# Out-projection of a Mamba-style mixer: three float32r passes from high and low parts in place of plain float32

## Chip, cores and metric
One NeuronCore of one Trainium2 chip runs the whole two-layer model in one launch. The metric is the device time of one launch in microseconds (us), the median of several runs; lower is better.

## What is computed
Two layers over 2 x 1024 tokens of width 256. The change touches one piece, the mixer of layer 0 (64 heads of 64 channels, 8 groups, 128 states). Cut to what matters:

```python
proj = einsum('bld,pd->blp', hidden, W_in)              # gate | x,B,C | dt
hbc  = silu(causal_conv4(x,B,C) + conv_b)
dt   = softplus(dt + dt_bias); A = -exp(A_log)
# per chunk: Y = (C B^T * L) (x dt) + C state * exp(cumsum(dt A));  state = decay * state + B^T (x dt decay)
y    = Y + D * x
g    = y * silu(gate)                                   # (tokens, 4096)
gg   = g.reshape(..., 8, 512); gg = gg * rsqrt(mean(gg*gg, -1) + EPS)
out  = (gg.reshape(..., 4096) * norm_weight) @ W_out.T  # the out-projection, (tokens, 256)
```

## The kernel before
`mixer` (L346 to L794) works group by group (8 groups of 512 channels), and in each group chunk by chunk (16 chunks of 128 tokens), so 128 chunks c. Five engines run five streams of instructions written out by hand, all as one loop over slots c = -5 to 130 (`SLOTS`, L430). In slot c the streams work on chunk c (its inputs), on p = c-1 (its output y) and on e = c-2 (its out-projection). Projection and convolution of x, B and C run ahead in 288 blocks spread over the slots (`fills`): two blocks a slot, three in every fourth slot. A block is 260, 384 or 388 columns wide.

TensorE (L540) in a slot: the state's part of y (L574), the diagonal part (L581), a block (L75 to L77 through `matmul3`), the gate's projection into the bank pgt, then four transposes of x into the bank pxt (L602), B and C (L608, L609), first half of the decay matrix `decays(c, 0)` (L563), state matmul (L619), the last block, `decays(c, 1)`, the out-projection of e (L632) and four transposes of y(p) into pxt (L640). `decays(c, 0)` waits for the rows rl and ll of chunk c, which SyncE loads from DRAM (`cs_in`, L559).

The out-projection: y is turned into pxt, ScalarE copies the bank to gt in float32 (L672), and TensorE multiplies gt by wo, four plain float32 matmuls of 128x128 by 128x256. TensorE carries each out as two instructions in the profile, so 8 a chunk, 1024 in all. VectorE adds the result to the accumulator (L794).

VectorE (L743) in a slot: t1 from the state's part (L748), `finish` of the last block of the slot before (L741), y (L759, it waits for GpSimd's addition L513 to t1), `taps` and `finish` of a block (L734, L741), the gate (L764, L767), the carry (L776), the decay matrix (L784), the last block's taps, the accumulation (L794). Where p is a multiple of 8, L748 is left out and y starts from xd.

GpSimd (L468) in a slot: L513, in slots 4 to 12 of a group one piece of `split` for the next group's weights, then L520, L523, L525, L530, and the two small operations L535 and L537. `split` makes high and low float32r parts of w_raw in pieces 0 to 7; piece 8, in slot 12, writes wo = wo_raw * norm weight into one of two buffers (L490) and raises `wo_split`.

SyncE (L438) is one queue in order. Per chunk it waits until the decays of chunk c-2 are done and issues four small loads, one of rl and three of ll (L462, L464). Ahead of those of chunk 16g+2 it waits for all three of `wx_split`, `wg_split` and `wo_split` of group g and loads the next group's weights, w_raw (1280 KB) and wo_raw (512 KB):

```python
if c % 16 == 2 and g < G0 - 1:      # L455
    sp.wait_ge(wx_split, 2 * (g + 1))
    sp.wait_ge(wg_split, 2 * (g + 1))
    sp.wait_ge(wo_split, g + 1)
    load_weights(g + 1)
```

Of the kernel before, what the change touches and what calls it, by code (L numbers as in the profile page):

```python
# [14 lines left out]
P = 128  # L15
T = 2048
D = 256
# [328 lines left out]
def mixer(nc, w_in, conv_w, conv_b, d_skip, norm_w, w_out, XH, XL, cs3, sel_rows, one_rows,  # L346
# [5 lines left out]
    with ExitStack() as ctx:  # L352
# [2 lines left out]
        w_raw = s.sb("w_raw", [P, KD, NXBC + GX])  # L355
        wx_hi, wx_lo = (s.sb(n, [P, 2, KD, NXBC], F32R) for n in ("wx_hi", "wx_lo"))
        wg_hi, wg_lo = (s.sb(n, [P, 2, KD, GX], F32R) for n in ("wg_hi", "wg_lo"))
        wo_raw, wo = s.sb("wo_raw", [P, GX // P, D]), s.sb("wo", [P, 2, GX // P, D])
        cw, cb = s.sb("cw", [P, G0, NCT, 4]), s.sb("cb", [P, G0, NCT])
        nw, dsk = s.sb("nw", [P, INTER // P]), s.sb("dsk", [P, H0])  # L360
        cv = s.sb("cv", [P, NCT, T // 2])
        xtok, xdt, xdtd, xd, t1, y, gt = (
            [s.sb(f"{n}{j}", [P, GX]) for j in range(2)] for n in ("xtok", "xdt", "xdtd", "xd", "t1", "y", "gt"))
        btok = [s.sb(f"btok{j}", [P, N0]) for j in range(2)]
        lm = [s.sb(f"lm{j}", [P, GH, Q]) for j in range(2)]
        tg, carry, decayed = (s.sb(n, [P, GX]) for n in ("tg", "carry", "decayed"))
# [7 lines left out]
        tabs_in, const, made, self_v, made_v = (s.sem(n) for n in ("tabs_in", "const", "made", "self_v", "made_v"))  # L374
        w_in_s, wx_split, wg_split, wo_split, hi_made = (
            s.sem(n) for n in ("w_in", "wx_split", "wg_split", "wo_split", "hi_made"))
        cs_in = [s.sem(f"cs_in{j}") for j in range(2)]
        (proj_done, xt_done, misc_done, d_done, yd_done, yo_done, s_done, gate_done, gt_done, op_done) = (
            s.sem(n) for n in ("proj_done", "xt_done", "misc_done", "d_done", "yd_done", "yo_done", "s_done",
# [37 lines left out]
        def fills(slot):  # L417
            return list(range(fill_at(slot), fill_at(slot + 1)))
# [13 lines left out]
        def wait(eng, sem, n):  # L432
            if n > 0:
                eng.wait_ge(sem, n)

        with nc.Block() as block:
# [30 lines left out]
            @block.gpsimd  # L467
            def _(pool):  # L468
                pool.memset(half[:, :], -0.5).then_inc(self_v, 1)

                pool.memset(eps_sum[:, :], 4 * EPS * GX).then_inc(self_v, 1)
                pool.memset(zero[:, :], 0.0).then_inc(self_v, 1)
                pool.wait_ge(tabs_in, 64)
                pool.tensor_scalar(nw[:, :], nw[:, :], float(GX) ** 0.5, None, ALU.mult).then_inc(self_v, 1)
                pool.wait_ge(self_v, 4)

                def split(g, piece):

                    o = g % 2
                    if piece < 4:  # L480
                        k = piece // 2
                        raw, hi, lo = w_raw[:, k, 0:NXBC], wx_hi[:, o, k, :], wx_lo[:, o, k, :]
                        done, at, cols = wx_split, 4 * g + k + 1, NXBC
                    elif piece < 8:
                        k = piece // 2 - 2
                        raw, hi, lo = w_raw[:, k, NXBC:], wg_hi[:, o, k, :], wg_lo[:, o, k, :]
                        done, at, cols = wg_split, 4 * g + k + 3, GX
                    else:
                        wait(pool, op_done, 16 * (g - 1))
                        pool.tensor_tensor(wo[:, o, :, :], wo_raw[:, :, :],  # L490
                                           nw[:, g * (GX // P):(g + 1) * (GX // P)].unsqueeze(2).to_broadcast([P, GX // P, D]),
                                           ALU.mult).then_inc(wo_split, 1)
                        return
                    if piece == 0:
                        pool.wait_ge(w_in_s, 32 * (g + 1))
                        wait(pool, proj_done, 36 * (g - 1))
                    if piece == 4:
                        wait(pool, gate_done, 16 * (g - 1))
                    if piece % 2 == 0:
                        pool.tensor_tensor(hi, raw, zero[:, :].to_broadcast([P, cols]), ALU.add).then_inc(hi_made, 1)  # L500
                    else:
                        pool.wait_ge(hi_made, at)
                        pool.tensor_tensor(lo, raw, hi.bitcast(F32), ALU.subtract).then_inc(done, 1)

                for piece in range(9):
                    split(0, piece)
                for c in SLOTS:
                    p = c - 1
                    if 0 <= p < NC and p % CPS:

                        pool.wait_ge(t1_done, n_off(p))
                        pool.wait_ge(xd_done, p + 1)
                        pool.tensor_tensor(t1[p % 2][:, :], t1[p % 2][:, :], xd[p % 2][:, :], ALU.add).then_inc(t1x_done, 1)  # L513
                    if 0 <= c < NC and 4 <= c % 16 < 13 and c // 16 < G0 - 1:
                        split(c // 16 + 1, c % 16 - 4)
                    if 0 <= c < NC:
                        o = c % 2
                        pool.wait_ge(xtok_ready, c + 1)
                        wait(pool, yd_done, c - 1)
                        pool.tensor_tensor(by_head(xdt[o]), by_head(xtok[o]), heads(TDT, c), ALU.mult).then_inc(xdt_done, 1)  # L520
                        if c % CPS < CPS - 1:
                            wait(pool, s_done, n_state(c - 2))
                            pool.tensor_tensor(by_head(xdtd[o]), by_head(xtok[o]), heads(TDTD, c), ALU.mult).then_inc(xdtd_done, 1)  # L523
                        wait(pool, y_done, c - 1)
                        pool.tensor_tensor(by_head(xd[o]), by_head(xtok[o]),  # L525
                                           dsk[:, c // 16 * GH:(c // 16 + 1) * GH].unsqueeze(2).to_broadcast([P, GH, HP]),
                                           ALU.mult).then_inc(xd_done, 1)
                        if 0 < c % CPS < CPS - 1:
                            pool.wait_ge(carry_done, n_off(c))
                            pool.tensor_tensor(by_head(decayed), by_head(carry), heads(DCH, c), ALU.mult).then_inc(cd_done, 1)  # L530
                    if 0 <= p < NC:
                        o = p % 2
                        pool.wait_ge(sq_done, p + 1)
                        wait(pool, acc_done, p - 1)
                        pool.tensor_tensor(rs[o][:, :], ss[o][:, :], eps_sum[:, :], ALU.add).then_inc(rs_v, 1)  # L535
                        pool.wait_ge(rs_v, p + 1)
                        pool.tensor_tensor(rs[o][:, :], rs[o][:, :], half[:, :], ALU.pow).then_inc(rs_done, 1)  # L537

            @block.tensor
            def _(pe):  # L540
# [27 lines left out]
                for c in SLOTS:  # L568
# [27 lines left out]
                    if live:  # L596
                        done = c // CPS * NB18 + SEG_OF[c % CPS] * NCT

                        pe.wait_ge(conv_done, done + NX)
                        wait(pe, gts_done, c - 1)  # L600
                        for k in range(NX):
                            last = pe.transpose(pxt[:, k * P:(k + 1) * P], cv[:, k, cols_of(c)], ident[:, :])  # L602
                        last.then_inc(xt_done, 1)

                        pe.wait_ge(conv_done, done + NCT)
                        wait(pe, btok_ready, c)
                        wait(pe, m_done, c)
                        pe.transpose(pmisc[:, 0:N0], cv[:, CT_B, cols_of(c)], ident[:, :])  # L608
                        pe.matmul(pmisc[:, N0:N0 + Q], cv[:, CT_B, cols_of(c)], cv[:, CT_C, cols_of(c)], start=True,  # L609
                                  stop=True).then_inc(misc_done, 1)  # L610
                        decays(c, 0)
# [12 lines left out]
                    if 0 <= e < NC:  # L624

                        pe.wait_ge(gts_done, e + 1)
                        pe.wait_ge(z_done, min(e + 2, NC))
                        wait(pe, acc_done, e)
                        if e % 16 == 0:
                            pe.wait_ge(wo_split, e // 16 + 1)  # L630
                        for k in range(NX):
                            last = pe.matmul(pgt[:, 0:D], gt[e % 2][:, k * P:(k + 1) * P], wo[:, e // 16 % 2, k, :],  # L632
                                             start=k == 0, stop=k == NX - 1)
                        last.then_inc(op_done, 1)
                    if 0 <= p < NC:

# [7 lines left out]
            def _(act):  # L644
# [21 lines left out]
                for c in SLOTS:  # L666
                    ks, live, p, e = fills(c), 0 <= c < NC, c - 1, c - 2
                    o = c % 2
                    if 0 <= e < NC:
                        act.wait_ge(gt_done, e + 1)  # L670
                        wait(act, op_done, e - 1)
                        act.activation(gt[e % 2][:, :], pxt[:, :], ACT.Copy).then_inc(gts_done, 1)  # L672
                    if len(fills(c - 1)) > 1:
                        squash(fills(c - 1)[-1])
                    if ks:
# [34 lines left out]
            def _(dve):  # L710
# [32 lines left out]
                for c in SLOTS:  # L743
# [4 lines left out]
                        dve.tensor_tensor(by_head(t1[o]), by_head(pyos), heads(TE1, p), ALU.mult).then_inc(t1_done, 1)  # L748
                    if len(fills(c - 1)) > 1:
                        finish(fills(c - 1)[-1])  # L750
                    if 0 <= p < NC:
                        if p % CPS:
                            dve.wait_ge(t1x_done, n_off(p))
# [1027 lines left out]
```

## Time and profile before

| | us |
|---|---|
| runs | 2948.06, 2948.74, 2952.24 (median 2948.74) |
| the profiled execution | 2949.92, span 2948.2 |
| mixer's loop, about | 380 to 1740 |

| engine | busy over the span |
|---|---|
| TensorE matmul | 2591.4 (88%) |
| VectorE | 2095.3 (71%) |
| ScalarE | 1211.8 (41%) |
| GpSimd | 1139.5 (39%) |

The profiled execution took 1.7 us beside its span. The mixer's 128 chunks are 46% of the span. L75 to L77 are the lines of `matmul3`, a helper used by all stages, so its groups are told apart by the tiles they write. PE is TensorE's matmul, PEld its weight load, DVE is VectorE, ACT ScalarE, POOL GpSimd, SPq SyncE's queue of DMA issues. Neighbouring matmuls overlap in the records, so what one costs is read from start to start.

### The profile page before, as it was taken

The numbers are of one execution on the slowest core, as the hardware profiler recorded it, in microseconds if no ns is written. First come the engines' busy times: TensorE is split into PE (matmuls) and PEld (weight loads), VectorE is DVE, ScalarE is ACT, GpSimd is POOL, SyncE is SP. The second block draws the span as 40 slices with busy tenths as digits, with TensorE's granted clock in tenths as the row PEclk, the third lists the DMA queues.
The fourth block names the chain that finished last, engine by engine and source line by source line (L and its number), as shares of the span: only waits on it lengthen the run. The fifth ranks groups of instructions, "written<-read, shape, count | busy, mean of one in ns | idle before, by whom it ended". The sixth has DMA issues, their size and how long they took to land. (4 is left out here: it accounts for less than half of the span.)

```text
span 2948.2 us, 44171 instructions
## 1 busy us (share of the span) xinstructions
PE 2591.4 (88%) x14212; PEld 1911.2 (65%) x14212; DVE 2095.3 (71%) x3431; ACT 1211.8 (41%) x2468; POOL 1139.5 (39%) x1240
## 2 busy tenths in 40 slices
PE   4894289999999999999999943999999869999993
PEld 2783278888888888888888832888888633333322
DVE  3355678888888888888888855777777664444434
ACT  1122145555555555555555521222222234444441
POOL 0251146565665656565665521455445200000000
PEclk9997589999999999999999976999999879999996
DMA  3100200000000000000000010000000031111114
GB/s 117 42 17 31 70 2 3 28 3 28 3 3 28 3 28 3 28 3 28 3 3 3 3 58 25 18 28 26 24 24 24 25 99 36 37 37 37 37 27 96
DMA packets 82365, 83.65 MB, mean 28 GB/s; under 512 B 25120, under 2 KB 71040, under 8 KB 79904
## 3 DMA queue, kind: packets, MB, share of 16 engines
q1 hardware_dynamic: 80672, 81.48, 9.4%
q8 instruction: 84, 1.38, 0.2%
q14 instruction: 73, 0.60, 0.1%
q10 hardware_dynamic: 1536, 0.20, 0.0%
HBM read 62.42 MB, written 16.78 MB: 27 GB/s over the span
## 5 line engine op out<-in xcount | busy, mean ns | idle before, releaser
L734 DVE SCALAR_TENSOR_TENSOR mix_cv<-mix_pp,mix_cw,mix_cv 128x384 f32<-128x384 f32 (+4 forms) x864 | 493.0, 571 | 25.4 <-ACT mix_cv L657 4.5
L1495 DVE TENSOR_REDUCE att_tops<-att_psc 128x1 f32<-128x512 f32 (+3 forms) x384 | 202.1, 555 | 219.3 <-PE att_psc L1433 131.8
L965 POOL TENSOR_TENSOR ffn_hl<-ffn_h,ffn_hh 128x512 fp32r<-128x512 f32 x144 | 186.2, 1293 | 319.6 <-ACT ffn_hh L1023 319.6
L1470 PE MATMUL att_po<-att_pr,att_vh 128*17 128x512 f32 (+3 forms) x768 | 290.6, 489 | 0.0
L581 PEld LDWEIGHTS mix_pyd<-mix_xdt,mix_lm 128*128 128x128 f32 x2048 | 249.1, 193 | 56.7 <-issue 53.1
L1534 ACT ACTIVATE att_pr<-att_pst 128x512 f32<-128x512 f32 (+3 forms) x384 | 175.8, 489 | 250.9 <-PE att_pst L1452 247.5
L75 PE MATMUL mix_pp<-l0in_XH,mix_wx_lo 128*128 128x384 f32 (+2 forms) x576 | 238.5, 414 | 36.3 <-DVE mix_ss L723 20.2
L657 ACT ACTIVATE mix_cv<-mix_pp,mix_cb,mix_cw 128x384 f32<-128x384 f32 (+1 forms) x288 | 182.4, 633 | 210.2 <-PE mix_pp L77 210.2
L632 PE MATMUL mix_pgt<-mix_wo,mix_gt 128*128 128x256 f32 x1024 | 244.9, 382 | 2.9 <-issue 2.2
L581 PE MATMUL mix_pyd<-mix_xdt,mix_lm 128*128 128x64 f32 x2048 | 244.4, 273 | 2.5 <-DVE mix_lm L784 2.5
L520 POOL TENSOR_TENSOR mix_xdt<-mix_xtok,l_dt 128x512 f32<-128x512 f32 x128 | 133.8, 1045 | 278.8 <-ACT mix_xtok L684 278.8
L1039 DVE SCALAR_TENSOR_TENSOR ffn_h<-ffn_th,ffn_pg 128x512 f32<-128x512 f32 x144 | 99.1, 688 | 197.5 <-ACT ffn_th L1018 197.5
L513 POOL TENSOR_TENSOR mix_t<-mix_t,mix_xd 128x512 f32<-128x512 f32 x112 | 144.5, 1290 | 218.9 <-DVE mix_t L748 138.7
L1023 ACT ACTIVATE ffn_hh<-ffn_h 128x512 fp32r<-128x512 f32 x144 | 91.4, 635 | 296.7 <-DVE ffn_h L1046 249.0
L632 PEld LDWEIGHTS mix_pgt<-mix_wo,mix_gt 128*128 128x128 f32 x1024 | 184.1, 190 | 31.2 <-issue 9.2
L663 ACT ACTIVATE mix_pp<-mix_cv 128x384 f32<-128x384 f32 (+1 forms) x288 | 133.0, 462 | 162.1 <-DVE mix_cv L734 160.7
L1018 ACT ACTIVATE ffn_th<-ffn_pg 128x512 f32<-128x512 f32 x144 | 86.5, 600 | 267.3 <-PE ffn_pc L995 147.5
L77 PE MATMUL mix_pp<-l0in_XH,mix_wx_hi 128*128 128x384 f32 (+2 forms) x576 | 188.1, 327 | 0.0
L76 PE MATMUL mix_pp<-l0in_XL,mix_wx_hi 128*128 128x384 f32 (+2 forms) x576 | 187.9, 326 | 0.0
L75 PE MATMUL ffn_po<-ffn_dh,ffn_hl 128*128 128x256 f32 x576 | 180.8, 314 | 7.6 <-DVE l_F L1053 4.3
L784 DVE TENSOR_TENSOR mix_lm<-mix_lm,mix_pmisc 128x1024 f32<-128x1024 f32 x128 | 156.1, 1220 | 23.0 <-ACT mix_lm L698 21.4
L75 PEld LDWEIGHTS mix_pp<-l0in_XH,mix_wx_lo 128*128 128x128 f32 x576 | 111.6, 194 | 85.6 <-DVE mix_cv L741 38.4
(292 smaller groups left out, 6712.6 us busy)
## 6 DMA issues: line engine op xcount, KB each, us to landing
mix_w_raw<-in_w_in SPq DMA_DIRECT2D x8, 1280.0 KB, 5.9
ffn_raw<-in_wgu SPq DMA_DIRECT2D x56, 128.0 KB, 2.2
mix_ll<-cs SPq DMA_DIRECT2D x384, 4.0 KB
att_qs<-q SPq DMA_DIRECT2D x192, 32.0 KB
mix_wo_raw<-in_w_out SPq DMA_DIRECT2D x8, 512.0 KB, 6.7
ffn_draw<-in_wd SPq DMA_DIRECT2D x28, 128.0 KB, 2.1
q<-qkv_part SPq DMA_DIRECT2D x24, 128.0 KB, 1.9
k<-qkv_part SPq DMA_DIRECT2D x24, 128.0 KB, 1.9
```

The lines of the kernel that those rows point to most:

```text
L75: pe.matmul(out, l_lo, r_hi, start=start, stop=False)
L76: pe.matmul(out, l_hi, r_lo, start=False, stop=False)
L77: return pe.matmul(out, l_hi, r_hi, start=False, stop=stop)
L581: last = pe.matmul(pyd[:, h * HP:(h + 1) * HP], lm[p % 2][:, h, :], xdt[p % 2][:, h * HP:(h + 1) * HP], start=True, stop=True)
L632: last = pe.matmul(pgt[:, 0:D], gt[e % 2][:, k * P:(k + 1) * P], wo[:, e // 16 % 2, k, :], start=k == 0, stop=k == NX - 1)
L657: act.activation(conv_tile(k), pp[k % 2][:, halo:cols], ACT.Identity, bias=cb[:, it // 2, ct:ct + 1], scale=cw[:, it // 2, ct, 3:4]).then_ ...
L734: last = dve.scalar_tensor_tensor(out, of, cw[:, g, ct, 3 - d:4 - d], out, ALU.mult, ALU.add)
L784: dve.tensor_tensor(lm[c % 2][:, :, :], lm[c % 2][:, :, :], pmisc[:, N0:N0 + Q].unsqueeze(1).to_broadcast([P, GH, Q]), ALU.mult).then_inc( ...
L965: pool.tensor_tensor(hl[u % NH][:, :], h[u % 2][:, :], hh[u % NH][:, :].bitcast(F32), ALU.subtract).then_inc(lo_done, 1)
L1470: last = pe.matmul(po[half][0:DH + 1, q0 - half * 512:q1 - half * 512], vh[(a + 1) % 2][:, kt, :], pr[(a + 1) % 2][:, at:at + q1 - q0], st ...
L1495: dve.tensor_reduce(tops[o][:, col:col + 1], psc[g % 2][:, 0:end - c], AX.X, ALU.max).then_inc(mx_done, 1)
L1534: act.activation(pr[a % 2][:, at:at + q1 - q0], pst[g % 3][:, 0:q1 - q0], ACT.Exp).then_inc(ex_done, 1)
```

## The change
The out-projection is computed as lo*hi + hi*lo + hi*hi of float32r parts. ScalarE's copy of pxt writes the high part gt_hi; VectorE subtracts it from the bank and writes the low part gt_lo, a new operation of 128x512 behind `finish` and ahead of y. The transposes of x and the out-projection now wait for it (`gtl_done`). The weights: piece 8 scales wo_raw in place (`wo_scaled`), and a new `split_out(g)` on GpSimd makes wo_hi and wo_lo, in one buffer each instead of wo's two, as the first thing in GpSimd's slot 16g+2, when the out-projections of group g-1 are done. Group 0 has it ahead of the slots. `wo_split` is raised by the second operation of `split_out`; the program of SyncE is as it was.

```diff
-        wo_raw, wo = s.sb("wo_raw", [P, GX // P, D]), s.sb("wo", [P, 2, GX // P, D])
+        wo_raw = s.sb("wo_raw", [P, GX // P, D])
+        wo_hi, wo_lo = (s.sb(n, [P, GX // P, D], F32R) for n in ("wo_hi", "wo_lo"))
...
+        gt_hi, gt_lo = ([s.sb(f"{n}{j}", [P, GX], F32R) for j in range(2)] for n in ("gt_hi", "gt_lo"))
...
-                        wait(pool, op_done, 16 * (g - 1))
-                        pool.tensor_tensor(wo[:, o, :, :], wo_raw[:, :, :],
+                        pool.tensor_tensor(wo_raw[:, :, :], wo_raw[:, :, :],
                                            nw[:, g * (GX // P):(g + 1) * (GX // P)].unsqueeze(2).to_broadcast([P, GX // P, D]),
-                                           ALU.mult).then_inc(wo_split, 1)
+                                           ALU.mult).then_inc(wo_scaled, 1)
...
+                def split_out(g):
+
+                    pool.wait_ge(wo_scaled, g + 1)
+                    wait(pool, op_done, 16 * g)
+                    pool.tensor_tensor(wo_hi[:, :, :], wo_raw[:, :, :], zero[:, :].unsqueeze(2).to_broadcast([P, GX // P, D]),
+                                       ALU.add).then_inc(wo_high, 1)
+                    pool.wait_ge(wo_high, g + 1)
+                    pool.tensor_tensor(wo_lo[:, :, :], wo_raw[:, :, :], wo_hi[:, :, :].bitcast(F32), ALU.subtract).then_inc(wo_split, 1)
+
                 for piece in range(9):
                     split(0, piece)
+                split_out(0)
                 for c in SLOTS:
                     p = c - 1
+                    if 18 <= c < NC and c % 16 == 2:
+                        split_out(c // 16)
...
-                        wait(pe, gts_done, c - 1)
+                        wait(pe, gtl_done, c - 1)
...
+                        pe.wait_ge(gtl_done, e + 1)
                         for k in range(NX):
-                            last = pe.matmul(pgt[:, 0:D], gt[e % 2][:, k * P:(k + 1) * P], wo[:, e // 16 % 2, k, :],
-                                             start=k == 0, stop=k == NX - 1)
+                            chans = slice(k * P, (k + 1) * P)
+                            last = matmul3(pe, pgt[:, 0:D], gt_hi[e % 2][:, chans], gt_lo[e % 2][:, chans], wo_hi[:, k, :],
+                                           wo_lo[:, k, :], k == 0, k == NX - 1)
...
-                        act.activation(gt[e % 2][:, :], pxt[:, :], ACT.Copy).then_inc(gts_done, 1)
+                        act.activation(gt_hi[e % 2][:, :], pxt[:, :], ACT.Copy).then_inc(gts_done, 1)
...
+                    if 0 <= e < NC:
+                        dve.wait_ge(gts_done, e + 1)
+                        dve.tensor_tensor(gt_lo[e % 2][:, :], pxt[:, :], gt_hi[e % 2][:, :].bitcast(F32), ALU.subtract).then_inc(gtl_done, 1)
```

## Rows read from the trace of the kernel before

**Rows 1.** Stretch: PE, PEld, DVE, ACT, POOL busy (count), PE clock, DMA share, GB/s.
```profile
380.00:1740.00 1360.00, 1321.65 (x7885) 1097.21 (x7884) 1174.44 (x1990) 741.67 (x1587) 796.21 (x895) 0.99 0.04 13
```

**Rows 2.** Timeline of PE: start us, us, operation, count, [idle before]; one out-projection.
```profile
1000.07 1.89 PE L632 MATMUL mix_pgt<-mix_wo,mix_gt 128*128 128x256 f32 x8
1001.80 0.60 PE L640 MATMUL mix_pxt<-all_ident,mix_y 128*128 128x128 f32 x4
```

**Rows 3.** Timeline of PE in a later stage: 12 float32r matmuls, 256 wide.
```profile
2000.49 0.45 PE L75 MATMUL ffn_po<-ffn_dh,ffn_hl 128*128 128x256 f32 x1
2000.78 0.28 PE L76 MATMUL ffn_po<-ffn_dl,ffn_hh 128*128 128x256 f32 x1
...
2002.07 0.40 PE L75 MATMUL ffn_pg<-l_XH,ffn_wl 128*128 128x512 f32 x1
```

**Rows 4.** Timeline of DVE: slot with p=8n, then slots with 384-wide blocks.
```profile
1070.38 0.68 DVE L759 TENSOR_TENSOR mix_y<-mix_pyd,mix_xd 128x512 f32<-128x512 f32 x1
...
1075.23 1.22 DVE L784 TENSOR_TENSOR mix_lm<-mix_lm,mix_pmisc 128x1024 f32<-128x1024 f32 x1 [0.40 <-ACT mix_lm L698]
...
1102.43 1.91 DVE L734 SCALAR_TENSOR_TENSOR mix_cv<-mix_pp,mix_cw,mix_cv 128x383 f32<-128x383 f32 x3
...
1112.07 0.69 DVE L759 TENSOR_TENSOR mix_y<-mix_pyd,mix_t 128x512 f32<-128x512 f32 x1 [0.93 <-POOL mix_t L513]
1112.68 1.91 DVE L734 SCALAR_TENSOR_TENSOR mix_cv<-mix_pp,mix_cw,mix_cv 128x383 f32<-128x383 f32 x3
```

**Rows 5.** Tiles w_raw and wo_raw: POOL's operations, ns min/median/max, first and last start.
```profile
L503 POOL TENSOR_TENSOR mix_wx_lo<-mix_w_raw,mix_wx_hi x16: 1844/1846/2062, 347.7 to 1469.0; 128x768 fp32r<-128x768 f32 x16
L503 POOL TENSOR_TENSOR mix_wg_lo<-mix_w_raw,mix_wg_hi x16: 1271/1276/1302, 354.7 to 1510.0; 128x512 fp32r<-128x512 f32 x16
L490 POOL TENSOR_TENSOR mix_wo<-mix_wo_raw,mix_nw x8: 1892/1896/1897, 358.3 to 1521.9; 128x1024 f32<-128x1024 f32 x8
```

**Rows 6.** Timeline, all engines: slots 16 to 18, where group 1 begins.
```profile
552.24 0.36 SPq L445 DMA_DIRECT2D mix_w_raw<-in_w_in  x1
...
561.53 0.26 SPq L462 DMA_DIRECT2D mix_rl<-cs  x1
...
573.17 0.55 POOL L537 TENSOR_TENSOR mix_rs<-mix_rs,mix_half 128x1 f32<-128x1 f32 x1
...
574.87 1.29 POOL L513 TENSOR_TENSOR mix_t<-mix_t,mix_xd 128x512 f32<-128x512 f32 x1 [1.16 <-DVE mix_t L748]
...
578.01 0.38 PE L563 MATMUL mix_pd<-mix_rl,mix_ll 96*128 96x256 bf16 x2
578.23 1.02 PE L619 MATMUL mix_pyos<-mix_xdtd,mix_btok 128*128 128x512 f32 x2
```

**Rows 7.** DMA issues: line, count, KB each, median us from issue to landing.
```profile
mix_w_raw<-in_w_in SPq DMA_DIRECT2D x8, 1280.0 KB, 5.9
mix_wo_raw<-in_w_out SPq DMA_DIRECT2D x8, 512.0 KB, 6.7
```

**Rows 8.** Timeline, the mixer's start: loads issued behind the first weights.
```profile
339.09 0.32 SPq L451 DMA_DIRECT2D mix_y<-in_c_one_rows  x1
...
346.11 1.47 POOL L500 TENSOR_TENSOR mix_wx_hi<-mix_w_raw,mix_zero 128x768 fp32r<-128x768 f32 x1 [5.02 <-DMA mix_wo_raw<-in_w_out]
347.23 0.50 DVE L718 CAST mix_ll<-mix_y 96x256 bf16<-96x256 f32 x1 [1.93 <-DMA mix_y<-in_c_one_rows]
```

**Rows 9.** Timeline of PE after two idle times in later stages.
```profile
1780.30 0.80 PE L75 MATMUL route_pl<-l_XH,route_wl 128*128 128x512 f32 x1 [5.06 <-DVE route_wl L1175]
...
1785.58 0.40 PE L75 MATMUL route_pl<-l_XH,route_wl 128*128 128x512 f32 x1
...
1830.53 0.79 PE L75 MATMUL ffn_pg<-l_XH,ffn_wl 128*128 128x512 f32 x1 [9.68 <-POOL ffn_dl L956]
...
1833.26 0.46 PE L75 MATMUL ffn_pu<-l_XH,ffn_wl 128*128 128x512 f32 x1
```

**Rows 10.** Columns of rows 1, for matmuls between the first two of rows 9.
```profile
1781.00:1785.00 4.00, 4.00 (x11) 3.17 (x10) 0.00 (x0) 0.60 (x1) 0.00 (x0) 0.50 0.00 0
```

More of the change, by code:

```diff
@@ L361, in mixer @@
         cv = s.sb("cv", [P, NCT, T // 2])
-        xtok, xdt, xdtd, xd, t1, y, gt = (
-            [s.sb(f"{n}{j}", [P, GX]) for j in range(2)] for n in ("xtok", "xdt", "xdtd", "xd", "t1", "y", "gt"))
+        xtok, xdt, xdtd, xd, t1, y = (
+            [s.sb(f"{n}{j}", [P, GX]) for j in range(2)] for n in ("xtok", "xdt", "xdtd", "xd", "t1", "y"))
+        gt_hi, gt_lo = ([s.sb(f"{n}{j}", [P, GX], F32R) for j in range(2)] for n in ("gt_hi", "gt_lo"))
         btok = [s.sb(f"btok{j}", [P, N0]) for j in range(2)]
@@ L376, in mixer @@
             s.sem(n) for n in ("w_in", "wx_split", "wg_split", "wo_split", "hi_made"))
+        wo_scaled, wo_high, gtl_done = s.sem("wo_scaled"), s.sem("wo_high"), s.sem("gtl_done")
         cs_in = [s.sem(f"cs_in{j}") for j in range(2)]
```

## Prediction
> **What bounds the kernel now.** I began with the busy time of the mixer's loop [rows 1]: of 1360 us TensorE is busy 97%, VectorE 86%, ScalarE 55%, GpSimd 59%, at a granted clock of 0.99. Next comes the timeline of VectorE, because 86% is an average over slots of different kinds [rows 4]. In a slot with 384-wide blocks the time from the taps behind one y (1102.43) to those behind the next (1112.68) is 10.25 us, and the only listed pause in it is 0.93 us, in which y waits for GpSimd's addition to t1, itself released by VectorE's t1. That pause is a fixed latency of VectorE's own chain. So in these slots VectorE is already at its floor, beside a TensorE that is nearly full. The whole loop shows its length in SyncE's rows: loads of the next group's weights are 16 slots apart, and chunk 18's rows are loaded at 561.53, 16.5 us before `decays(18, 0)` reads them at 578.01 [rows 6]. That lead hides the load today, and it is this lead that the change touches.
>
> **TensorE's part.** An out-projection starts at 1000.07 and the next operation at 1001.80: 1.73 us for 8 instructions [rows 2]. The same shape in float32r, 12 matmuls of 128x128 by 128x256, stands in the feed-forward stage: 2000.49 to 2002.07 is 1.58 us, of which the first step takes 0.29 and the other eleven 0.117 each [rows 3]. I take 1.58, since it is the same group with its opening. TensorE saves 0.15 us a chunk, 19 us over 128; without any opening cost (12 x 0.117 = 1.40) it would be 0.33, or 42 us. A page's price stands by itself: the Trainium skill (TensorE: Matmul & The Clock Gate, Back-to-back issue gap) gives columns / 2.4 + 2.5 ns, an estimate of 109 ns for 256 columns, by which twelve would take 1.31 us and the saving would be 54 us; the row, at 117 ns plus an opening, is slower and decides.
>
> **VectorE's part.** gt_lo is one 128x512 operation reading a bank, like y, which takes 0.69 us and from start to next start 0.61 [rows 4]. It stands behind `finish` and ahead of y, in the pause of 0.93, so it costs nothing in seven slots of eight. If ScalarE's copy came late, or y's addend early, that cover would be gone, and each slot would pay up to 0.61. Where p is a multiple of 8 there is no t1 and no such pause: y at 1070.38 starts without a wait [rows 4], and 0.61 is added to it, against a pause of 0.40 later in the slot at 1075.23. That is up to 0.2 a time. Because VectorE's floor holds in the 384-wide slots, I keep only part of TensorE's saving: in the five lighter or mixed slots of eight 0.15 each, in the three heaviest nothing, less 0.2 to 0.3, so about 0.5 per eight chunks, 16 x 0.5 = 8 us. The ends are -19 (all of it) and +5 (the floor takes all and the slots of the eighth kind pay).
>
> **GpSimd's part.** `split_out` is new: two operations of 1024 columns, fp32r. The high part is like L490 with a broadcast operand, 1.90 us. The low part from its two sizes: 1.85 at 768 and 1.28 at 512 columns give 2.22 ns a column, so 2.42 us [rows 5]. Together 4.32, and with their hand-over 4.4. It stands first in slot 16g+2, when L537 of the slot before ends at 573.72 [rows 6]; it ends at 578.1. L513, now at 574.87, and so y, the gate and xdtd for the state matmul (578.23) come 3.3 us late. The scaling in slot 12 stays as it is. For group 0 all is done ahead of the slots: the loads of group 1 start 4.4 us later there, 16 slots before they are used, and nothing waits. The wait for the out-projections of the group before holds nothing, as the last is through by then.
>
> **SyncE's queue, the term that decides.** SyncE must see `wo_split` of group g before it issues the next weights and, behind them in the same queue, the four loads of chunk 16g+2. Today it passes at 552.24, because that signal came in slot 12 of the group before. Now the signal comes at 578.1, inside the very slot that needs the chunk's rows. From there: w_raw is issued at 578.2, wo_raw 0.4 later and lands 6.7 after that, at 585.3 [rows 6, 7]. Do the small loads behind wait for the big ones? At the mixer's start the last constant is issued behind the first weights at 339.09 and lands 8.1 us later, at 347.2, 1.1 us after wo_raw (346.1) [rows 8]. So the chunk's rows land 0.3 to 1.1 us behind 585.3, say at 585.9, and `decays(18, 0)` moves from 578.01 to 585.9: 7.9 us. TensorE executes in order, so the state matmul, the last block, the out-projection and all behind wait with it. GpSimd's 3.3 us run out inside this stall. The bounds: 4.3 us if small loads slip past big ones (six issues of about 0.35 put the last one at 580.3, and I allow 2 for a small load alone, an estimate, well under the 5.9 of w_raw [rows 7]), and 10 if the landing is as late as at the start (8.1 behind a last issue begun at 579.9).
>
> **The clock.** After 9.68 us of idle time TensorE's first six matmuls stand 0.455 apart, and after 5.06 twelve stand 0.44 apart [rows 9], where the granted clock is 0.50 [rows 10], its lower level of 1.2 GHz. The mixer's stretch stands at 0.99 [rows 1]. So 2.7 to 5.3 us of work at half speed follow such a pause: half of that is lost, 1.4 to 2.6, I take 2.1. The bounds are 0 (the stall ends before the clock falls) and 3.
>
> **The sum.** There are six such places, groups 1 to 6 (chunks 18, 34, 50, 66, 82, 98): 6 x (7.9 + 2.1) = 60. Chunk 114 has no load to wait for; there GpSimd's 3.3 us show, 3. Less 8. Together +55 us on the profiled execution's 2949.9, so 3004.9; the median of the runs is 1.2 lower, and I give 3004.
>
> **The rivals.**
> Small loads slip past the weights. For it: four loads of 4 to 6 KB need no bandwidth. Against: the start of the mixer. Six stalls of 4.3, too short for a clock loss in most, give 26 + 3 - 8 = +21: 2970. Chance 0.14.
> VectorE is the bound. The subtraction isn't covered (ScalarE's copy of pxt comes late behind its other work), and each slot pays about 0.5: 64 us in place of the gain of 8, on top of the stalls: +127, 3076. For it: the 384-wide slots have one pause only; against: that pause, 0.93, lies in front of exactly this place [rows 4]. Chance 0.05.
> The other side, faster. GpSimd gets `split_out` in before the chunk's rows are needed and the queue is passed in time. Its place is the order of slot 16g+2 and its price is the whole gain kept, -8 to -19, so 2930 to 2941. It decides only if `wo_split` rises some 8 us before `decays(16g+2, 0)`; in the rows it rises 0.1 after. For it speaks that GpSimd idles 41% of the time; against, that the operations stand behind slot 16g+1's last two in program order. Chance 0.04.
> The loads' stall absent but GpSimd's delay felt in seven places: 7 x 3.3 - 8 = +15, 2964: chance 0.03.
>
> **How the numbers follow.** The forecast has 0.74. Its own range is six stalls of 7 to 10 with a clock loss of 1 to 3, plus 3, less 8 to 0: about 2991 to 3030. With the first rival taken in, the range is 2966 to 3032. A measurement of this kernel tells about 0.2% (6 us) from no change. Faster by more than that: 0.04. Within it: 0.03. Slower: 0.93.
>
> **What would show it.** In SyncE's timeline, w_raw of groups 2 to 7 issued behind GpSimd's new low part, 25 us later in its slot than today, and the loads of rl and ll right behind. In TensorE's waits, L563 released by a DMA six times, 7 to 9 us each, and the matmuls behind it at the lower clock. L513 3.3 us late in slot 114. The out-projection at 1.58 us from start to start. VectorE's pause before y shrunk from 0.93 to about 0.3. It is wrong if no wait of TensorE for a DMA is over 3 us, if the small loads land well ahead of wo_raw, or if groups without a weight load also lengthen.

## The result and the profile after

| | before | after |
|---|---|---|
| median, us | 2949.17 | 3001.06 |
| runs, lowest to highest | 2948.06 to 2952.24 | 3000.45 to 3008.64 |
| ratio to before, 95% interval | | 1.018 (1.0162 to 1.0198) |
| span of the profiled execution | 2948.2 | 2998.8 |

The median before is over four runs, one more than in the table of the kernel before. The change made the kernel slower by 1.8%. The page of the kernel after opens with the busy time and the count of each engine:

```profile
span 2998.8 us, 45467 instructions
PE 2577.6 (86%) x14724; PEld 1909.8 (64%) x14724; DVE 2164.5 (72%) x3559; ACT 1212.5 (40%) x2468; POOL 1174.0 (39%) x1256
```

TensorE is busy 13.8 us less than before, with 512 instructions more. VectorE has its 128 subtractions more (69 us), GpSimd 16 operations. TensorE did no more work, so the 50 us are time in which it stood, or worked at a lower clock. Its waits over the mixer, longest in total first (us in total, times, longest):

```profile
PE mix_pd L577 <- DMA mix_ll<-cs: 45.0, 6, 7.8
PE mix_pd L577 <- ACT mix_lm L709: 25.4, 32, 2.5
PE mix_pp L75 <- DVE mix_cv L757: 16.4, 30, 0.8
```

The first row did not exist before: the decay matmuls wait for a load, six times, 7.5 us on average. The timeline of all engines shows the first of them, where group 1 begins; [rows 6] are the same place before:

```profile
572.17 1.90 POOL L511 TENSOR_TENSOR mix_wo_hi<-mix_wo_raw,mix_zero 128x1024 fp32r<-128x1024 f32 x1
...
574.14 2.40 POOL L514 TENSOR_TENSOR mix_wo_lo<-mix_wo_raw,mix_wo_hi 128x1024 fp32r<-128x1024 f32 x1
...
576.49 1.27 POOL L527 TENSOR_TENSOR mix_t<-mix_t,mix_xd 128x512 f32<-128x512 f32 x1
576.62 0.36 SPq L448 DMA_DIRECT2D mix_w_raw<-in_w_in  x1
...
577.02 0.43 SPq L449 DMA_DIRECT2D mix_wo_raw<-in_w_out  x1
577.50 0.30 SPq L465 DMA_DIRECT2D mix_rl<-cs  x1
...
584.38 0.61 PE L577 MATMUL mix_pd<-mix_rl,mix_ll 96*128 96x256 bf16 x2 [7.75 <-DMA mix_ll<-cs]
```

GpSimd ends the low part at 576.5, SyncE issues the weights 0.1 us later and the chunk's rows behind them, and TensorE, ready at 576.6, goes on at 584.4. Behind that the clock is at its lower level, then back (windows of the same trace; columns as in [rows 1]):

```profile
584.40:587.00 2.60, 2.60 (x7) 1.50 (x8) 0.27 (x1) 0.60 (x1) 0.00 (x0) 0.50 0.00 0
588.00:592.00 4.00, 4.00 (x32) 3.52 (x31) 3.31 (x6) 2.63 (x6) 1.28 (x3) 1.00 0.02 5
```

Away from these places the slots got shorter. SyncE issues the rows rl of chunk c when the decays of chunk c-2 are done, so its issues are a clock of the loop. Those of chunks 105 and 113, before:

```profile
1474.99 0.23 SPq L462 DMA_DIRECT2D mix_rl<-cs  x1
...
1559.06 0.23 SPq L462 DMA_DIRECT2D mix_rl<-cs  x1
```

and after:

```profile
1524.67 0.23 SPq L465 DMA_DIRECT2D mix_rl<-cs  x1
...
1608.21 0.23 SPq L465 DMA_DIRECT2D mix_rl<-cs  x1
```

Eight chunks took 84.07 us and take 83.54: 0.53 less. The other eights of chunks without a group's beginning, from chunk 9 on, gained 0.46 to 0.56. I call the time of such eight chunks the rhythm. From group to group the issues of the kernel after fall behind those of before by 7.9 to 8.8 us, 50.6 over groups 1 to 6; with the 1.06 gained in each, one group's beginning costs 9.5. In group 7, which has no load to wait for, it costs 2.8. The account: 6 x 9.5 + 2.8 - 16 x 0.53 = 51.3, and the last chunk's issue stands 50.4 behind.

### The profile page after: what moved, and what is told of

It reads as the page before. It is cut to its first block and busy times, and to the rows that moved or that the text cites. A ratio compares the mean times of both kernels' runs of the same rounds, so it can differ in the third digit from the quotient of the medians.

```text
span 2998.8 us, 45467 instructions
## 1 busy us (share of the span) xinstructions
PE 2577.6 (86%) x14724; PEld 1909.8 (64%) x14724; DVE 2164.5 (72%) x3559; ACT 1212.5 (40%) x2468; POOL 1174.0 (39%) x1256
## 5 line engine op out<-in xcount | busy, mean ns | idle before, releaser
L577 PE MATMUL mix_pd<-mix_rl,mix_ll 96*128 96x256 bf16 x512 | 102.0, 281 | 70.4 <-DMA mix_ll<-cs 45.0
L76 PE MATMUL ffn_po<-ffn_dl,ffn_hh 128*128 128x256 f32 x576 | 162.0, 281 | 0.0
```

The costliest lines, as they stand in the source:

```text
L76: pe.matmul(out, l_hi, r_lo, start=False, stop=False)
```

## The experiments

Theory A is that of the prediction: SyncE's wait for `wo_split`, and the chunk's rows behind the weights in its queue, make the stalls. Rival B: GpSimd's two operations ahead of L513 do. Rival C: small loads slip past big ones. Ratios are to the kernel before on the same chip; its median there was 2946.42 for e1 to e4 and 2949.67 for e5 to e8. So a run of e5 to e8 is set against e3 by the two ratios or by the rhythm, not by the two medians. The loop's part of a difference is read from the rhythm.

**e1_rows_first: the same wait, the other order in the queue.**

```diff
                         sp.wait_ge(wo_split, g + 1)
-                        load_weights(g + 1)
                     wait(sp, d_done, 2 * (c - 1))
...
+                    if c % 16 == 2 and g < G0 - 1:
+                        load_weights(g + 1)
```

> SyncE still waits for the split of the out-projection's weights, but then issues the chunk's four small loads ahead of w_raw and wo_raw. Theory A (the queue: the chunk's rows wait for the signal, and then behind 1.8 MB of weights): the wait for the signal stays, the queueing goes; TensorE's six waits for the rows shrink from 7.3 to 7.8 us to about 3.3 (four issues 1.3 plus a small load's landing of 2), and the clock no longer falls: 3001 - 6 x 6 = about 2965. Rival B (GpSimd's 4.4 us ahead of its addition hold TensorE, and the load is only the last to arrive): the time stays near 3001. Rival C (small loads slip past big ones anyway): no change, 3001.

Measured: 2965.51, ratio 1.006 (1.0043 to 1.0077). Timeline at the same place:

```profile
575.07 0.23 SPq L464 DMA_DIRECT2D mix_rl<-cs  x1
...
576.36 0.36 SPq L448 DMA_DIRECT2D mix_w_raw<-in_w_in  x1
...
577.40 0.39 PE L578 MATMUL mix_pd<-mix_rl,mix_ll 96*128 96x256 bf16 x2 [2.39 <-DMA mix_ll<-cs]
```

The wait is 2.4 us in place of 7.5, with SyncE's signal as late as it was. So the small loads do stand behind the 1.8 MB, and C falls. B falls as the whole story, too: GpSimd's program is unchanged. A page agrees: the Trainium skill (DMA: Bandwidth & Descriptors, Queues, rings and completion order) says that within one queue each DMA engine takes up descriptors in the order of its ring. A theory to correct, though: the clock still fell, against the expectation (a window of the same trace, from 576 to 584 us):

```profile
576.00:584.00 8.00, 6.60 (x33) 5.12 (x34) 6.58 (x12) 3.16 (x7) 4.94 (x7) 0.79 0.67 238
```

It fell at six of the seven groups' beginnings. At the one where it did not, group 4, TensorE's wait was as long as at the others:

```profile
1090.68 0.39 PE L578 MATMUL mix_pd<-mix_rl,mix_ll 96*128 96x256 bf16 x2 [2.41 <-DMA mix_ll<-cs]
```
```profile
1090.70:1094.70 4.00, 3.96 (x26) 3.07 (x27) 3.93 (x7) 2.57 (x6) 2.52 (x3) 1.00 0.95 346
```

By SyncE's issues that beginning cost 2.8, and the six others 3.9 to 4.4.

**e2_weights_behind: the rows of the chunk are issued without the wait.** The block of L455 stands behind the four small loads instead of ahead of them.

```diff
-                    if c % 16 == 2 and g < G0 - 1:
-                        sp.wait_ge(wx_split, 2 * (g + 1))
-                        sp.wait_ge(wg_split, 2 * (g + 1))
-                        sp.wait_ge(wo_split, g + 1)
-                        load_weights(g + 1)
                     wait(sp, d_done, 2 * (c - 1))
...
+                    if c % 16 == 2 and g < G0 - 1:
+                        sp.wait_ge(wx_split, 2 * (g + 1))
+                        sp.wait_ge(wg_split, 2 * (g + 1))
+                        sp.wait_ge(wo_split, g + 1)
+                        load_weights(g + 1)
```

> SyncE issues the rows of chunk 16g+2 without waiting, then waits for the three splits and loads the weights. Theory A: TensorE's waits for a load vanish, and in groups 1 to 6 only GpSimd's delay is left, which group 7 shows at 2.8 us: 3001 - 6 x (9.5 - 2.8) = about 2961. Rival B: near 3001, as GpSimd's two operations stand where they stood.

Measured: 2968.78, ratio 1.0073 (1.0056 to 1.009). No wait of TensorE for a load is left in the mixer, and SyncE's issues fall behind by 2.7 a group: 3.8 with the 1.06 gained, not 2.8. TensorE's wait is now on GpSimd's delay, which reaches it through y, VectorE's taps, ScalarE's tanh and its exponential:

```profile
580.77 0.51 PE L577 MATMUL mix_pd<-mix_rl,mix_ll 96*128 96x256 bf16 x2 [2.54 <-ACT mix_lm L709]
```

and the clock falls behind even this short wait, here and at all seven beginnings:

```profile
581.20:583.90 2.70, 2.70 (x13) 2.70 (x13) 2.67 (x5) 1.66 (x4) 1.71 (x3) 0.50 0.57 215
```

In the changed kernel's group 7 the same wait of 2.5 us was followed by a clock of 1.00:

```profile
1639.63 0.39 PE L577 MATMUL mix_pd<-mix_rl,mix_ll 96*128 96x256 bf16 x2 [2.51 <-ACT mix_lm L709]
```
```profile
1640.00:1643.00 3.00, 2.96 (x22) 2.49 (x21) 2.93 (x6) 2.27 (x5) 1.75 (x3) 1.00 0.03 6
```

That fits the difference of 3.8 and 2.8, and so do e2's own group 7, which has the same waits but the lower clock and costs 3.6, and group 4 of e1. So of the 9.5 us that a group's beginning costs, the queue makes 5.7, and 3.8 would be left of GpSimd's two operations alone, its clock loss with it. e1 and e2 stand within each other's intervals: the late signal costs little once the weights are not ahead of the rows.

**e3_split_early: neither wait nor delay.** Two buffers for wo_hi and wo_lo; the high part is made in slot 13 and the low part in slot 14 of the group before, each behind L513, where `split`'s pieces stand. Room for it came from gt_hi and gt_lo with one buffer each, the squares written over xdt, and the columns of one element in one tile.

```diff
-        wo_hi, wo_lo = (s.sb(n, [P, GX // P, D], F32R) for n in ("wo_hi", "wo_lo"))
+        wo_hi, wo_lo = (s.sb(n, [P, 2, GX // P, D], F32R) for n in ("wo_hi", "wo_lo"))
...
-                    if 18 <= c < NC and c % 16 == 2:
-                        split_out(c // 16)
...
+                    if 0 <= c < NC and 13 <= c % 16 < 15 and c // 16 < G0 - 1:
+                        split_out(c // 16 + 1, c % 16 - 13)
```

> High and low weights in two buffers each, made in slots 13 and 14 of the group before, one operation a slot; SyncE's program as in the changed kernel. Room for it: one buffer for gt_hi and gt_lo each, and the squares are written over xdt. Theory A with GpSimd's part: neither a stall nor a delay is left, only the gain of 0.53 us per eight chunks: 2949 - 8 = about 2941. Rival D (the new VectorE operation holds the slots back and the gain is not real outside of the stalls): 2949 or more.

Measured: 2938.31, ratio 0.9977 (0.9966 to 0.9987): 8.1 us less than before. GpSimd's low part, the one at issue, now ends at 535, and SyncE passes as early as it did before the change:

```profile
532.67 2.39 POOL L517 TENSOR_TENSOR mix_wo_lo<-mix_wo_raw,mix_wo_hi 128x1024 fp32r<-128x1024 f32 x1
```
```profile
550.34 0.36 SPq L448 DMA_DIRECT2D mix_w_raw<-in_w_in  x1
```

The three passes with their subtraction are therefore a small gain, 0.2% (0.1 to 0.3), and the whole loss came from where the weights' split stands. The edits that made room did little to the loop: its rhythm is 83.48, beside 83.54 in the change.

**e4_low_part_only: VectorE's operation beside plain float32.** The kernel before, with the subtraction from the bank and both waits for it.

```diff
+                    if 0 <= e < NC:
+                        dve.wait_ge(gts_done, e + 1)
+                        dve.tensor_tensor(gt_lo[e % 2][:, :], pxt[:, :], gt[e % 2][:, :], ALU.subtract).then_inc(gtl_done, 1)
```

> The kernel before with VectorE's subtraction and the two waits for it, its result unused; the out-projection stays plain float32. If VectorE's pause ahead of y covers the subtraction in seven slots of eight (forecast), 2949 + 16 x 0.2 to 0.4 = about 2952 to 2955. If the subtraction costs its 0.6 us in every slot, about 3026.

Measured: 2958.53, ratio 1.0038 (1.0026 to 1.0051). The median is 12.1 above, and more than the 2952 to 2955 expected. The rhythm grew by 0.48 us per eight chunks, 7.7 over the loop, about twice what the forecast had for it, and far from 0.6 a slot. The other 4 us lie outside the rhythm; their cause stays open.

The next four ask what bounds the slots now. Theory F: VectorE's chain t1, GpSimd's L513, y is the floor of the slots with 384-wide blocks. Rivals: G (the subtraction costs the same everywhere), H (TensorE bounds all slots), I (VectorE bounds all).

**e5_no_low_part: three passes without the subtraction.** e3 without VectorE's operation; gt_hi stands in for gt_lo.

```diff
-                        dve.tensor_tensor(gt_lo[:, :], pxt[:, :], gt_hi[:, :].bitcast(F32), ALU.subtract).then_inc(gtl_done, 1)
...
-                            last = matmul3(pe, pgt[:, 0:D], gt_hi[:, chans], gt_lo[:, chans],
+                            last = matmul3(pe, pgt[:, 0:D], gt_hi[:, chans], gt_hi[:, chans],
```

> As e3_split_early, but VectorE's subtraction is left out and TensorE multiplies the high part twice in its place (the low part of the activations is not computed). Theory F (in slots with 384-wide blocks the floor is VectorE's chain t1, GpSimd's addition, y, and the subtraction lies inside its pause): only the slots with p a multiple of 8 gain, 0 to 3 us, 2935 to 2938. Rival G (the subtraction costs the same everywhere as it did beside plain float32, 8 to 12 us): 2926 to 2930.

Measured: 2935.04, ratio 0.9954 (0.9937 to 0.997); its interval overlaps that of e3. In the rhythm it is 0.26 us under e3 over chunks 105 to 113 and 0.37 over chunks 9 to 17, so 4 to 6 us over the loop: between F and G. Nearly all of it is in one slot of eight, a light one (with 260-wide blocks), whose issues of rl stand 9.34 apart in place of 9.6. In the slots with 384-wide blocks, though, nothing changed: VectorE's y waits 0.94 us again, and stands 10.26 behind the one before, as with the subtraction.

```profile
1094.39 0.69 DVE L779 TENSOR_TENSOR mix_y<-mix_pyd,mix_t 128x512 f32<-128x512 f32 x1 [0.94 <-POOL mix_t L530]
1104.65 0.69 DVE L779 TENSOR_TENSOR mix_y<-mix_pyd,mix_t 128x512 f32<-128x512 f32 x1 [0.94 <-POOL mix_t L530]
```

**e6_two_passes: TensorE's third pass taken away.**

```diff
-                            last = matmul3(pe, pgt[:, 0:D], gt_hi[:, chans], gt_lo[:, chans],
-                                           wo_hi[:, e // 16 % 2, k, :], wo_lo[:, e // 16 % 2, k, :], k == 0, k == NX - 1)
+                            pe.matmul(pgt[:, 0:D], gt_lo[:, chans], wo_hi[:, e // 16 % 2, k, :], start=k == 0, stop=False)
+                            last = pe.matmul(pgt[:, 0:D], gt_hi[:, chans], wo_hi[:, e // 16 % 2, k, :], start=False,
+                                             stop=k == NX - 1)
```

> As e3_split_early with two passes of float32r instead of three (the product with the low part of the weights is left out): TensorE has 4 x 0.117 = 0.47 us less a chunk. Theory F: only the slots with 260-wide blocks can use it, up to about 0.3 in four slots of eight, 16 x 1.2 = 19: about 2919. Rival H (TensorE is the bound in every slot): 128 x 0.47 = 60 less, 2878. Rival I (VectorE bounds every slot): 2938, no change.

Measured: 2938.38, ratio 0.9963 (0.9951 to 0.9976). The rhythm is 0.13 to 0.23 us under e3's, about 3 over the loop. A third of the out-projection's matmuls is gone (the group takes 1.0 us in place of 1.5), and nearly nothing comes of it: H falls. F expected 19 and gave TensorE too much; of the numbers that of I, no change, is the nearest. But I as it was put, VectorE's work as the bound of every slot, does not fit e5, where 0.61 us less of its work a slot gave 4 to 6 us of 78. The time went into longer waits of TensorE for the others (e6, from 420 to 1700 us; in e3 the two rows read 22.4 and 16.0):

```profile
PE mix_pd L582 <- ACT mix_lm L715: 44.6, 60, 1.6
PE mix_pp L75 <- DVE mix_cv L763: 27.5, 30, 1.1
```

**e7_sum_behind_t1: VectorE's chain shortened.** e3 with the addition to the accumulator moved from the end of a slot to behind t1 in the next.

```diff
                         dve.tensor_tensor(by_head(t1[o]), by_head(pyos), heads(TE1, p), ALU.mult).then_inc(t1_done, 1)
+                    if 0 <= c - 3 < NC:
+                        last_e = c - 3
+                        dve.wait_ge(op_done, last_e + 1)
+                        dve.wait_ge(rs_done, last_e + 1)
+                        row = ACC[:, last_e // CPS % 2 * CPS + last_e % CPS, :]
+                        dve.scalar_tensor_tensor(row, pgt[:, 0:D], rs[last_e % 2][:, 0:1], row, ALU.mult, ALU.add).then_inc(acc_done, 1)
...
-                    if 0 <= e < NC:
-                        dve.wait_ge(op_done, e + 1)
...
```

> As e3_split_early, and VectorE's addition to the accumulator (0.39 us from start to start) moves from the end of a slot to behind t1 of the next, into the pause ahead of y. Theory F: t1 and so y come about 0.35 earlier against the operations before; the slots with 384-wide blocks shorten by about 0.3, four or five of eight: 16 x 1.2 = 19 less, about 2919. Rival H: no change, 2938.

Measured: 2913.75, ratio 0.9879 (0.9862 to 0.9895), 36 us less than the kernel before. By the two ratios that is 29 us below e3, by the rhythm 30 (1.89 per eight chunks), and 19 were expected. No work was taken away. VectorE's timeline in a slot with 384-wide blocks shows why:

```profile
1109.77 0.68 DVE L769 TENSOR_TENSOR mix_t<-mix_pyos,l_exp_cs 128x512 f32<-128x512 f32 x1
...
1110.37 0.48 DVE L775 SCALAR_TENSOR_TENSOR main_X<-mix_pgt,mix_few,main_X 128x256 f32<-128x256 f32 x1
...
1110.76 0.55 DVE L762 SCALAR_TENSOR_TENSOR mix_cv<-mix_pp,mix_cv 128x384 f32<-128x384 f32 x1
...
1111.22 0.68 DVE L780 TENSOR_TENSOR mix_gt_lo<-mix_pxt,mix_gt_hi 128x512 fp32r<-128x512 f32 x1
...
1111.86 0.69 DVE L789 TENSOR_TENSOR mix_y<-mix_pyd,mix_t 128x512 f32<-128x512 f32 x1
```

The addition, 0.39 from start to start, and the subtraction, 0.64, fill the time in which GpSimd adds to t1, and y has no wait left. Its issues of chunks 105 and 113 are 81.59 apart:

```profile
1444.32 0.23 SPq L465 DMA_DIRECT2D mix_rl<-cs  x1
...
1525.91 0.23 SPq L465 DMA_DIRECT2D mix_rl<-cs  x1
```

**e8_sum_behind_t1_plain: the same move in the kernel before.** The diff is that of e7.

> The same move in the kernel before, with plain float32. If TensorE is its bound in nearly all slots: 2940 to 2946. If VectorE's chain is (theory F for the kernel before, too): about 19 less, 2928.

Measured: 2935.35, ratio 0.9953 (0.9937 to 0.997), between the two expectations. y still has a wait, of 0.55, that nothing fills:

```profile
1103.78 0.69 DVE L765 TENSOR_TENSOR mix_y<-mix_pyd,mix_t 128x512 f32<-128x512 f32 x1 [0.55 <-POOL mix_t L513]
```

TensorE, though, hardly waits for anything between 420 and 1700 us, so I read it as the bound here; no run took work from it in this kernel:

```profile
PE mix_pd L563 <- ACT mix_lm L693: 8.3, 15, 0.6
PE mix_pp L75 <- DVE mix_cv L741: 3.2, 15, 0.2
```

The rhythm of all, chunks 105 to 113, in us:

| | sum at the slot's end | sum behind t1 |
|---|---|---|
| plain float32 | 84.07 (before) | 83.15 (e8) |
| plain float32 with the subtraction | 84.55 (e4) | |
| three passes | 83.48 (e3), 83.54 (the change) | 81.59 (e7) |
| three passes without the subtraction | 83.22 (e5) | |
| two passes | 83.32 (e6) | |

The three passes with their subtraction are worth 0.6 per eight chunks, 9 us over the loop, where the sum stands at the slot's end and VectorE's chain is the floor of the heavy slots (with 384-wide blocks). They are worth 1.56, 25 us, where the sum stands behind t1.

## Why the prediction was right

The forecast was 3004 with a range of 2966 to 3032; the median is 3001.06, and the likeliest case is what happened. Its terms measured 45.0 for the queue, 12 for the clock and 2.8 for group 7, less 8.5 for the gain: 51.3, where it had 47, 13, 3 and 8. Three of the four are right in mechanism and size. The gain has its size by luck, as told below. By its steps:

**SyncE's queue.** Forecast 7.9 us at each of six places, measured 7.5 (45.0 over six). Each link held: GpSimd's operations at 1.90 and 2.40 us (forecast 1.90 and 2.42), w_raw issued 0.1 behind, the rows behind the weights. e1 shows the last link by itself, e2 that the wait for a load goes when the rows are issued ahead of the signal.

**The clock.** Forecast 2.1 a stall; 9.5 less 7.5 leaves 2.0. In windows of half a microsecond of the same trace the clock stands at 0.50 for 2.9 to 5.5 us behind the six stalls, 4.1 on the mean, and half of that is 2.1. The rival that set the range's lower end took it that a wait of 4.3 us would mostly be too short for the clock to fall. That was wrong: it fell behind 2.4 to 2.6 us at thirteen of fourteen beginnings in e1 and e2, though not at one in e1 nor in the changed kernel's group 7.

**GpSimd's delay.** Forecast 3.3 in group 7 alone, measured 2.8, and hidden elsewhere by the stall, as said. What the prediction did not give is what it would cost by itself in the six other groups: 3.8 each, by e2. The rival with the stall absent had 3.3. Among its signs of being wrong the prediction also named that groups without a weight load lengthen; group 7 has none and does, as the sum itself says, so that sign was put too widely.

**The gain.** Forecast 0.5 per eight chunks, measured 0.53, but both of its terms were too small, and it came in other slots than forecast. TensorE's term was mis-sized: the out-projection takes 1.49 on the mean of the slots, in place of 1.75 before, so 0.26 less a chunk and not 0.15. Of these 2.1 us per eight chunks the loop got about 1.1 (e4 to e3, with the subtraction in both). The subtraction costs 0.48 per eight beside plain float32 and 0.26 to 0.37 beside float32r (e3 to e5), not 0.2 to 0.3. It was forecast that the light slots gain 0.15 each and the heavy ones nothing. In the issues of rl it is the reverse: two slots of eight with 384-wide blocks shorten by 0.31 and 0.14, one lengthens by 0.10, and the light ones shorten by 0.1 at most. What failed is the reading of the floor: the prediction took the 10.25 us of one heavy slot for all. VectorE's timeline before has the next two y 10.49 and 10.40 apart, above that floor; in the changed kernel both are 10.25 to 10.27:

```profile
1122.56 0.69 DVE L759 TENSOR_TENSOR mix_y<-mix_pyd,mix_t 128x512 f32<-128x512 f32 x1 [0.94 <-POOL mix_t L513]
...
1132.96 0.69 DVE L759 TENSOR_TENSOR mix_y<-mix_pyd,mix_t 128x512 f32<-128x512 f32 x1 [0.94 <-POOL mix_t L513]
```

The rest of TensorE's saving goes into its waits for VectorE. One of them the list of waits does not name stands ahead of the out-projection itself, which writes the bank pgt and so waits for VectorE's last reading of that bank, the product of y and the gate (L767 before, L786 after, `z_done`). A light slot before, from the timeline of all engines:

```profile
569.13 0.69 DVE L767 TENSOR_TENSOR mix_y<-mix_y,mix_pgt 128x512 f32<-128x512 f32 x1
...
570.09 0.39 PE L563 MATMUL mix_pd<-mix_rl,mix_ll 96*128 96x256 bf16 x2
...
570.32 1.89 PE L632 MATMUL mix_pgt<-mix_wo,mix_gt 128*128 128x256 f32 x8
...
572.05 0.60 PE L640 MATMUL mix_pxt<-all_ident,mix_y 128*128 128x128 f32 x4
```

and after:

```profile
568.22 0.69 DVE L786 TENSOR_TENSOR mix_y<-mix_y,mix_pgt 128x512 f32<-128x512 f32 x1
...
568.58 0.39 PE L577 MATMUL mix_pd<-mix_rl,mix_ll 96*128 96x256 bf16 x2
...
569.01 0.36 PE L75 MATMUL mix_pgt<-mix_wo_hi,mix_gt_lo 128*128 128x256 f32 x1
...
570.50 0.60 PE L656 MATMUL mix_pxt<-all_ident,mix_y 128*128 128x128 f32 x4
```

Before, VectorE's product ends at 569.82, half a microsecond ahead of the out-projection. After, it ends at 568.91 and the out-projection begins 0.10 later, so 0.43 behind the decay matmuls in place of 0.23: the group takes 1.49 in place of 1.73, but both together 1.92 in place of 1.96. The out-projection begins 0.1 behind the end of VectorE's product in 88 of 126 slots of the changed kernel and in 35 of 126 before. This is read from the timelines; no run moved that product. Where that product is early, in the changed kernel, the group begins 0.15 behind the decay matmuls. The page's estimate of 1.31 for the group, by the Trainium skill (TensorE: Matmul & The Clock Gate, Back-to-back issue gap), is for matmuls by themselves and is under the 1.49 that the trace shows.

**VectorE's pause.** Forecast to shrink from 0.93 to about 0.3; VectorE's timeline has 0.34, with the subtraction in front of it:

```profile
1154.09 0.68 DVE L769 TENSOR_TENSOR mix_gt_lo<-mix_pxt,mix_gt_hi 128x512 fp32r<-128x512 f32 x1
...
1155.11 0.69 DVE L778 TENSOR_TENSOR mix_y<-mix_pyd,mix_t 128x512 f32<-128x512 f32 x1 [0.34 <-POOL mix_t L527]
```

**The rivals.** That small loads slip past the weights is refuted by e1. That the subtraction is uncovered everywhere is refuted by e4 (8 us in the rhythm, 12 in the median, not 64). The faster side, split early enough, did not happen in the change; e3 built it, and its forecast of 2930 to 2941 held with 2938. The prediction named the split's place as the point from which it decides, and that is what the experiments show.

## What to carry to other kernels

Before moving a step that raises a signal, list every queue that waits for the signal and what stands behind that wait in program order: here a split moved by six slots cost 9.5 us a group. Of these 5.7 fell on unrelated rows, which shared SyncE's queue, and 3.8 came of its two operations standing ahead of GpSimd's addition to t1. Its own data came in time. Small loads that are needed soon go ahead of large ones in a queue. Where an engine waits for another engine's answer to its own last operation, look for work that stands elsewhere in the loop and can move into that wait: here one moved operation of 0.39 us gave some 30 us, where taking away a third of TensorE's out-projection gave 3. And before a saving on one engine is counted, list what its next step still waits for: here a bank that VectorE reads.

## What was not expected of the hardware

The granted clock fell to 0.50 behind waits of 2.5 us in e2, in a stream that had run at 0.99, at seven beginnings of seven, and stayed at 1.00 behind equal waits in group 4 of e1 and group 7 of the changed kernel. A pause of TensorE of that length can cost 1 us beyond itself, or nothing. And the four products of the out-projection take less time as twelve float32r matmuls (1.49 us) than as plain float32 (1.75).
